# A first feed-forward with eight gated experts: bias products on four row groups, second projection behind the last expert bank

## The chip, the cores and the metric

The kernel runs on one core of a Trainium2 chip. The metric is the device time of one execution in microseconds (us), the median over several runs; lower is better. TensorE is the matmul engine, VectorE, ScalarE and GpSimd are the elementwise engines (DVE, ACT and POOL in the rows), SyncE (SP) issues most transfers.

## The reference

A two-layer transformer on 4 x 512 tokens of width 256, float32. The change touches the first layer's feed-forward, a dense mixture of experts:

```python
router_logits = x @ router_w + router_b          # 8 experts
top 2 of softmax(router_logits), renormalised -> gates (zero for the others)
expert_out = gelu(einsum('bsh,ehd->ebsd', x, expert_w) + expert_b)
combined   = einsum('bse,ebsd->bsd', gates, expert_out)
y          = combined @ out_w + out_b
x          = layernorm(x + y)
```

Before it stands an attention with 16 heads of width 16, behind it an attention with 16 heads of width 128 in 4 groups, and a second feed-forward with a capacity per expert. All 8 experts are computed for every token; the gates pick two.

## The kernel before

**Numbers.** Each float32 matrix is split into two bfloat16 parts, high and low, and a product is three matmuls (`mm3`, lines 350 to 355: high by high, high by low, low by high). The profile shows them as lines 353, 354 and 355.

**Tiles.** The 2048 tokens are 16 tiles (NT) of 128. The 8 experts of a tile are 8 x 256 = 2048 columns, four PSUM banks of 512: banks 4 to 7, two experts in each. `experts(t, p)` (line 502) computes bank p of tile t: it waits until the gelu of the same bank of tile t-1 has read it (`m["ge"]`), issues one bias product (line 506) with three rows of ones against three bfloat16 parts of the bias, and then six matmuls of 512 columns (two halves of the 256 inputs, three parts each). The bias is in `eb3`, rows 0 to 2 of a scratch region, 2048 columns wide.

**What follows a bank.** ScalarE applies the gelu (`gelu`, line 942) into `ge[p]`. VectorE (`mix`, lines 1284 and 1287) weighs experts 0 to 4 with their gates and adds them up; GpSimd does experts 5, 6 and 7 (`mix`, lines 1593 and 1598); VectorE joins both sums (`join_halves`, line 1293). TensorE transposes the combined tile ("cm", line 468), ScalarE and VectorE copy the transposed tile into high and low parts (lines 803 and 1092), and `second_project` (line 485) multiplies it with the output weights: six matmuls of 256 columns into bank 3. VectorE adds the result to the rows and takes their statistics (`joined(t, 2)`, lines 1197 to 1200), GpSimd forms the inverse deviation (`inverse_deviation`, lines 1577 and 1580), VectorE scales (`norm(t, 2)`, line 1206), and TensorE transposes the new rows ("x2") for the next layer.

**Three tiles at once.** A loop over steps n (line 593; its engines have the same loop at lines 958, 1336 and 1601) works on the experts of tile n, the second projection of tile n-1, the x2 transposes of tile n-2, and far ahead on the end of the attention: the first projection and norm of tile n+6 (`first_project`, `joined(n + 6, 1)`, `norm(n + 6, 1)`), its transposes "x1" of tile n+5, and the transposes "cc" of tile n+7. Tiles ahead end with step 9. At n = 3, 7, 11 (and before 0) a step also routes four tiles: logits on TensorE, softmax and top 2 on VectorE, with a table load of ScalarE before and after the exponential.

**Order.** All engines are programmed by hand in program order, with semaphores between them. Within a step it is:
- TensorE: x1 transposes; bank 0; logits (routing steps); x2 transposes; first projection; bank 1; cm transposes; cc transposes; bank 2; second projection; bank 3.
- ScalarE: x1 copy; gelu 0; x2 copy; gelu 1; cm copy; cc copy; gelu 2; gelu 3.
- VectorE: x1, x2 low parts; mix 0; joined(n+6, 1); cm, cc low parts; mix 1; norm(n+6, 1); joined(n-1, 2); mix 2; context; norm(n-1, 2); join_halves(n).
- GpSimd: inverse deviation for norm 1; mix 2; inverse deviation for norm(n-1, 2); mix 3; adding the output bias to rows (line 1618).

A turn waits until the low part of the turn before the last has been read (`hold(pe, m["tlo"], i - 1)`), so in a full step the cm transposes wait for join_halves and for the x1 low part behind it.

Step 16 has no experts: it starts the next layer's K, Q and V projections (`l1_project`), and the second projection of tile 15 stands before V. Step 17 holds the x2 transposes of tile 15. Then come the next layer's scores (line 646).

**The bias.** SyncE loads it as 16 rows of 128, GpSimd splits it into three parts (`eb_p`), and three copies by DMA (line 328) lay each part out as one row of 2048. TensorE waits for them at line 563, after the first attention.

Of the kernel before, what the change touches and what calls it, by code (L numbers as in the profile page):

```python
# [6 lines left out]
BF16 = mybir.dt.bfloat16  # L7
# [10 lines left out]
NT = NB * TT  # L18
# [105 lines left out]
def build(nc, x_tok_d, x_t_d, wqkv_d, wall_d, const_d, bp_d, outb_d, b2_d, rb_d, eb_d, rw0_d, rw1_d, b1_d, out_d):  # L124
    ctx = ExitStack()
    with ctx:
        def sb(name, shape, dt=F32):
            return ctx.enter_context(nc.sbuf_tensor(name, shape, dt))

        def sem(name):  # L130
            return ctx.enter_context(nc.semaphore(name))
# [12 lines left out]
        scr = sb("scr", [P, 16384])  # L144
# [5 lines left out]
        ones_b = sb("ones_b", [P, P], BF16)  # L150
# [52 lines left out]
        eb_f = scr[0:16, 6400:6528]  # L203
        eb_p = scr[0:16, 6528:6720].bitcast(BF16).rearrange("p (i d) -> p i d", i=3)
        eb_r = scr[0:16, 6720:6976].rearrange("p (i d) -> p i d", i=2)
        eb3 = scr[0:3, 15360:16384].bitcast(BF16)

        def tiles(base, n, width, dt=F32):
            return [scr[:, base + width * i:base + width * (i + 1)].bitcast(dt) if dt != F32
                    else scr[:, base + width * i:base + width * (i + 1)] for i in range(n)]  # L210
# [7 lines left out]
        ge = tiles(8192, 4, 512)  # L218
# [10 lines left out]
        bank = [ctx.enter_context(nc.psum_tensor(f"bank{i}", [P, 512], F32)) for i in range(8)]  # L229
# [12 lines left out]
        eb_moved = sem("eb_moved")  # L242
# [11 lines left out]
        def hold(eng, semaphore, value):  # L254

            if value > 0:
                eng.wait_ge(semaphore, value)

        def group_sems(p):
# [7 lines left out]
        m = {n: sem(f"mix_{n}") for n in (  # L267
            "rc", "cc", "tp", "thi", "tlo", "o1", "o2", "r1", "r2", "agg1", "agg2", "rstd1", "rstd2", "x1", "x2", "xb",
            "lg", "lgc", "lgd", "ex", "gates", "f", "ge", "mul", "pmul", "psum", "dve", "pool")}
# [21 lines left out]
        def _(sp):  # L291
# [32 lines left out]
            sp.wait_ge(ch_done, NCH)  # L324
            sp.dma_start(eb_f, eb_d).then_inc(ld_b, 16)
            sp.wait_ge(eb_ready, 1)
            for i in range(3):
                sp.dma_start(eb3[i:i + 1, :], eb_p[:, i, :]).then_inc(eb_moved, 16)

            def l1_turns(u):  # L330

# [18 lines left out]
        def _(pe):  # L350
# [134 lines left out]
            def second_project(t):  # L485
                pe.wait_ge(m["tlo"], TURNS.index(("cm", t)) + 1)
                hold(pe, m["r2"], t)
                project(bank[3][:, 0:E], tc_hi[t % 2], tc_lo[t % 2], OUTW).then_inc(m["o2"], 1)
# [12 lines left out]

            def experts(t, p):

                hold(pe, m["ge"], 4 * (t - 1) + p + 1)
                out = bank[4 + p][:, :]
                pe.matmul(out, ones_b[0:3, :], eb3[:, p * 512:(p + 1) * 512], start=True, stop=False)
                for k in range(KE):
                    cs = slice(EXPW + k * NX * E + p * 512, EXPW + k * NX * E + (p + 1) * 512)
                    last = mm3(out, tb_hi[t % TB][:, k * P:(k + 1) * P], tb_lo[t % TB][:, k * P:(k + 1) * P],
                               w_hi[:, cs], w_lo[:, cs], False, k == KE - 1)  # L510
                last.then_inc(m["f"], 1)
# [31 lines left out]
            for _ in range(WARM):  # L543
                pe.matmul(bank[7][:, :], ones_b[:, :], ones_b[:, :].unsqueeze(1).to_broadcast([P, TT, P]),
                          start=True, stop=True)
# [14 lines left out]


            pe.wait_ge(ch_done, NCH)
            pe.wait_ge(eb_moved, 48)
            pe.wait_ge(a["vc"], NH + 2)
            def l1_project(which, g, j=0):

# [26 lines left out]
            for n in STEPS[len(EARLY):]:  # L593
                here, ahead, behind = 0 <= n < NT, n + LEAD + 1, n - 1
                if 0 <= n + LEAD < NT:
                    turn_mix("x1", n + LEAD)
                if n == NT:

                    pe.wait_ge(m["ge"], 4 * NT)
                    l1_project("k", 0)  # L600
                if here:
                    experts(n, 0)
                if 0 <= n + 4 < NT and (n + 4) % TT == TT - 1:
                    logits((n + 4) // TT)
                if 0 <= n - 2:
                    turn_mix("x2", n - 2)

                routed = 0 <= n + 4 < NT and (n + 4) % TT == TT - 1
                if 0 <= ahead < NT and not routed:
                    first_project(ahead)  # L610
                if here:
                    experts(n, 1)
                if 0 <= ahead < NT and routed:
                    first_project(ahead)
                if 0 <= behind < NT:
                    turn_mix("cm", behind)
                if 0 <= n + LEAD + 2 < NT:
                    turn_mix("cc", n + LEAD + 2)
                if n == NT:
                    l1_project("q", 0, 0)  # L620
                if here:
                    experts(n, 2)
                if 0 <= behind < NT:
                    second_project(behind)
                if n == NT:
                    l1_project("v", 0)
                if here:
                    experts(n, 3)
            l1_project("q", 0, 1)


# [1067 lines left out]
```

## Time and profile before

| | |
|---|---|
| median of 3 runs | 1030.12 us (1030.11 to 1031.32) |
| the profiled execution | 1035.02 us, its span 1033.2 us |
| busy share of the span | TensorE 90%, VectorE 80%, ScalarE 61%, GpSimd 36% |
| mean granted TensorE clock | 0.973 |
| first attention | to 311.7 us |
| stage of the change, tile 0 to the next layer's scores | 324.4 to 497.3 us |
| starts of bank 0 of tiles 4, 5, 6, 7, 8 | 365.2, 378.0, 388.2, 398.6, 409.5 us |
| starts of bank 0 of tiles 12, 13, 14, 15 | 450.7, 461.2, 469.6, 477.9 us |

The starts of bank 0 are those of its bias products. A tile takes 10.4 us where a tile ahead is projected too, 12.8 with routing, and 8.4 at the end. In a row of the timeline the first number is the start in us from the span's start, the second the duration, then the engine, the line, the operation and what it writes and reads; a bracket tells how long the engine sat idle before it and who released it. The idle time of an engine that nobody waits for costs nothing.

### The profile page before, as it was taken

How to read it: one execution, taken by the hardware profiler on the slowest of the kernel's cores; microseconds unless marked ns; L12 is line 12 of the kernel's file. 1: busy time of each engine (PE TensorE's matmuls, PEld its weight loads, DVE VectorE, ACT ScalarE, POOL GpSimd, SP SyncE). 2: the span in 40 equal slices, each digit the busy share in tenths (PEclk: the TensorE clock that was granted, in tenths of full speed). 3: DMA queues.
4: the chain of work that ended last, by engine and by line, in shares of the span. 5: the costliest groups of instructions: out<-in, count | busy, mean ns of one | idle time of the engine just before them, and what ended most of it. 6: DMA issues, size and time to landing. Idle time of an engine off the chain costs nothing.

```text
span 1033.2 us, 23457 instructions
## 1 busy us (share of the span) xinstructions
PE 925.1 (90%) x8745; PEld 626.5 (61%) x8745; DVE 822.4 (80%) x2400; ACT 629.7 (61%) x1560; POOL 373.7 (36%) x605
## 2 busy tenths in 40 slices
PE   6888888887877988998899999999999999999996
PEld 4667676666663444433555566666666666667654
DVE  6999998989986687765799988888888888733566
ACT  6999998989862344343666655555555555432543
POOL 4333342530422545444233333333333333310085
PEclk8999999999986999999999999999999999999999
DMA  7202121100000000000266755555555655510001
GB/s 267 63 23 63 43 63 43 46 20 2 2 2 1 1 1 1 1 1 1 56 125 121 123 100 96 100 97 96 103 103 102 98 97 100 95 36 1 1 32 52
DMA packets 174626, 61.41 MB, mean 59 GB/s; under 512 B 169248, under 2 KB 170800, under 8 KB 174384
## 3 DMA queue, kind: packets, MB, share of 16 engines
q1 hardware_dynamic: 174512, 59.90, 28.7%
q8 instruction: 70, 1.15, 0.4%
q14 instruction: 44, 0.36, 0.1%
HBM read 15.83 MB, written 2.10 MB: 17 GB/s over the span
## 4 chain that ended last, share of the span: by engine, by line
PE 47%; DVE 31%; ACT 6%; POOL 5%; DMA 5%; issue 5%; SPq 0%; POOLq 0%; DVEq 0%; ACTq 0%
PE bank L353 11%; PE bank L355 11%; PE bank L354 11%; DVE s_sb L1135 7%; DMA pt_lo<-w_lo 5%; DVE pt_lo L1092 5%; DVE scr L1122 3%; DVE scr L1092 3%; PE bank L668 3%; PE bank L670 3%; PE bank L669 3%; DVE w_lo L1153 2%; ACT s_sb L850 2%; ACT scr L803 2%; POOL scr L1598 2%
## 5 line engine op out<-in xcount | busy, mean ns | idle before, releaser
L1135 DVE CUSTOM_DVE_ANT_0 s_sb<-bank,consts 128x512 f32<-128x512 f32 (+3 forms) x512 | 227.9, 481 | 23.3 <-PE bank L355 15.0
L852 ACT ACTIVATE s_sb<-s_sb,nm 128x512 f32<-128x512 f32 (+3 forms) x256 | 141.4, 553 | 103.8 <-DVE nm L1135 102.4
L353 PE MATMUL bank<-w_hi,scr 128*128 128x256 bf16 (+1 forms) x576 | 174.2, 302 | 5.1 <-DVE lg_sb L1299 2.6
L355 PE MATMUL bank<-w_hi,scr 128*128 128x256 bf16 (+1 forms) x576 | 173.6, 301 | 0.0
L354 PE MATMUL bank<-w_lo,scr 128*128 128x256 bf16 (+1 forms) x576 | 173.6, 301 | 0.0
L803 ACT ACTIVATE scr<-bank 128x256 bf16<-128x256 f32 (+4 forms) x256 | 120.2, 487 | 76.1 <-PE bank L670 44.5
L850 ACT ACTIVATE s_sb<-s_sb,nm 128x512 f32<-128x512 f32 (+3 forms) x256 | 141.2, 584 | 13.5 <-DVE nm L1135 13.4
L1628 POOL TENSOR_SCALAR wqkv_hi<-s_sb,rr 128x512 bf16<-128x512 f32 (+3 forms) x128 | 65.6, 532 | 141.7 <-DVE rr L1159 141.7
L1092 DVE TENSOR_TENSOR pt_lo<-bank,pt_hi 128x512 bf16<-128x512 f32 (+1 forms) x192 | 108.4, 592 | 7.6 <-ACT pt_hi L803 7.6
L1092 DVE TENSOR_TENSOR scr<-bank,scr 128x256 bf16<-128x256 f32 (+1 forms) x160 | 80.6, 525 | 40.8 <-ACT scr L803 40.4
L403 PE MATMUL bank<-scr 128*128 128x512 bf16 (+3 forms) x256 | 61.7, 306 | 50.9 <-DVE nm L1135 49.4
L1628 POOL TENSOR_SCALAR w_hi<-s_sb,rr 128x512 bf16<-128x512 f32 (+3 forms) x128 | 65.6, 532 | 105.2 <-DVE rr L1159 105.2
L803 ACT ACTIVATE pt_hi<-bank 128x512 bf16<-128x512 f32 (+1 forms) x192 | 96.4, 550 | 2.7 <-PE bank L449 2.7
L668 PE MATMUL bank<-pt_hi,w_hi 128*128 128x384 bf16 (+2 forms) x320 | 84.8, 275 | 10.6 <-DMA pt_lo<-w_lo 9.8
L942 ACT ACTIVATE scr<-bank 128x512 f32<-128x512 f32 x64 | 38.2, 597 | 86.0 <-PE bank L355 82.5
L669 PE MATMUL bank<-pt_lo,w_hi 128*128 128x384 bf16 (+2 forms) x320 | 87.9, 275 | 0.0
L353 PE MATMUL bank<-xt_hi,w_hi 128*128 128x512 bf16 x224 | 84.9, 379 | 1.7 <-ACT scr L1023 0.8
L355 PE MATMUL bank<-xt_hi,w_lo 128*128 128x512 bf16 x224 | 84.9, 379 | 0.0
L354 PE MATMUL bank<-xt_lo,w_hi 128*128 128x512 bf16 x224 | 84.9, 379 | 0.0
L670 PE MATMUL bank<-pt_hi,w_lo 128*128 128x384 bf16 (+2 forms) x320 | 84.6, 275 | 0.0
L353 PEld LDWEIGHTS bank<-w_hi,scr 128*128 128x128 bf16 x576 | 56.8, 99 | 43.3 <-issue 15.9
L449 PE MATMUL bank<-consts,s_sb 128*128 128x128 f32 x640 | 81.7, 275 | 0.0
(160 smaller groups left out, 2348.6 us busy)
## 6 DMA issues: line engine op xcount, KB each, us to landing
scr<-wall_in SPq DMA_DIRECT2D x19, 512.0 KB, 3.8
x_tok<-x_tok_in SPq DMA_DIRECT2D x1, 2048.0 KB, 9.8
scr<-x_t_in SPq DMA_DIRECT2D x3, 512.0 KB, 9.4
out<-x_tok SPq DMA_DIRECT2D x3, 512.0 KB, 2.6
scr<-wqkv_in SPq DMA_DIRECT2D x2, 384.0 KB, 4.0
pt_hi<-w_hi SPq DMA_TRANSPOSE x32, 3.3
pt_lo<-w_lo SPq DMA_TRANSPOSE x32, 3.4
pt_hi<-wqkv_hi SPq DMA_TRANSPOSE x32, 3.4
```

Of the source, the lines that this page charges most:

```text
L353: pe.matmul(out, l_hi, r_hi, start=start, stop=False, skip_group_check=check)
L354: pe.matmul(out, l_hi, r_lo, start=False, stop=False, skip_group_check=check)
L355: return pe.matmul(out, l_lo, r_hi, start=False, stop=stop, skip_group_check=check)
L668: pe.matmul(out, v1_hi[:, vs], hi, start=(kt, q0) == (0, 0), stop=False, skip_group_check=True)
L669: pe.matmul(out, v1_hi[:, vs], lo, start=False, stop=False, skip_group_check=True)
L670: last = pe.matmul(out, v1_lo[:, vs], hi, start=False, stop=(kt == TT - 1), skip_group_check=True)
L803: return act.activation(out, in_, ACT.Copy)
L850: last = act.activation(at, at, ACT.Exp, bias=nm[:, j % 2, qt:qt + 1], scale=-1.0)
L852: last = act.activation(at, at, ACT.Exp, bias=nm[:, j % 2, qt:qt + 1], scale=-1.0, accum_out=rs[:, j % 2, qt:qt + 1])
L1092: return dve.tensor_tensor(out, bank_cols, hi, ALU.subtract)
L1135: last = dve.tensor_tensor_reduce(s_sb[j % 2][:, S_OFF[qt]:S_OFF[qt] + w], bank[turn][:, col:col + w], mask[:, 512 - w:512], -scale, HUGE, ...
L1628: pool.tensor_scalar(ps_hi[j % 2][:, at], s_sb[j % 2][:, at], rr[:, j % 2, qt:qt + 1], 1.0, ALU.mult, ALU.mult).then_inc(c["row"], 1)
```

## The change

One bias product per bank becomes a group of four at the head of bank 0. The bias region is laid out anew: 12 row copies by DMA instead of three put the three parts of bank q's 512 columns into rows 32q to 32q+2, so that the four products read four different groups of 32 rows and are given the array's four row groups by `tile_position`. As all four banks are written at that point, bank 0 waits for all four gelus of the tile before (`4 * t`), and banks 1 to 3 for nothing. The second projection of the tile before is moved from between banks 2 and 3 to behind bank 3; in step 16 this puts it behind the V projection of the next layer.

```diff
-        eb3 = scr[0:3, 15360:16384].bitcast(BF16)
+        eb3 = scr[:, 15360:15616].bitcast(BF16)
...
-            for i in range(3):
-                sp.dma_start(eb3[i:i + 1, :], eb_p[:, i, :]).then_inc(eb_moved, 16)
+            for p in range(4):
+                for i in range(3):
+                    sp.dma_start(eb3[32 * p + i:32 * p + i + 1, :], eb_p[4 * p:4 * p + 4, i, :]).then_inc(eb_moved, 16)
...
             def experts(t, p):
 
-                hold(pe, m["ge"], 4 * (t - 1) + p + 1)
                 out = bank[4 + p][:, :]
-                pe.matmul(out, ones_b[0:3, :], eb3[:, p * 512:(p + 1) * 512], start=True, stop=False)
+                if p == 0:
+                    hold(pe, m["ge"], 4 * t)
+                    for q in range(4):
+                        rows = slice(32 * q, 32 * q + 3)
+                        pe.matmul(bank[4 + q][:, :], ones_b[rows, :], eb3[rows, :], start=True, stop=False,
+                                  tile_position=(32 * q, 0))
                 for k in range(KE):
...
-            pe.wait_ge(eb_moved, 48)
+            pe.wait_ge(eb_moved, 12 * 16)
...
                 if here:
                     experts(n, 2)
-                if 0 <= behind < NT:
-                    second_project(behind)
                 if n == NT:
                     l1_project("v", 0)
                 if here:
                     experts(n, 3)
+                if 0 <= behind < NT:
+                    second_project(behind)
```

## Rows read from the trace of the kernel before

**Rows 1.** The page, part 1: busy time, share of the span and instructions.
```profile
PE 925.1 (90%) x8745; PEld 626.5 (61%) x8745; DVE 822.4 (80%) x2400; ACT 629.7 (61%) x1560; POOL 373.7 (36%) x605
```
**Rows 2.** Waits, 324 to 486 us: who waited for whom, us, times, longest.
```profile
DVE scr L1293 <- POOL scr L1598: 29.9, 12, 3.5
```
**Rows 3.** Timeline of step 5, from one join_halves to the next.
```profile
381.77 0.93 DVE L1293 TENSOR_TENSOR scr<-scr 128x256 f32<-128x256 f32 x1 [2.37 <-POOL scr L1598]
...
383.18 0.74 PE L468 MATMUL bank<-consts,scr 128*128 128x128 f32 x4 [0.81 <-DVE scr L1092]
...
383.85 0.38 PE L506 MATMUL bank<-scr,ones_b 3*128 3x512 bf16 x1
...
384.17 0.39 PE L353 MATMUL bank<-w_hi,scr 128*128 128x512 bf16 x1
...
385.52 0.10 PEld L353 LDWEIGHTS bank<-w_hi,scr 128*128 128x128 bf16 x1 [0.38 <-DVE scr L1092]
...
386.08 0.27 PE L355 MATMUL bank<-w_hi,scr 128*128 128x256 bf16 x1
...
386.28 0.39 PE L506 MATMUL bank<-scr,ones_b 3*128 3x512 bf16 x1
...
387.12 0.40 DVE L1197 TENSOR_TENSOR x_tok<-bank,x_tok 128x256 f32<-128x256 f32 x1
...
389.42 0.61 POOL L1593 TENSOR_SCALAR scr<-scr,s_sb 128x256 f32<-128x256 f32 x1
...
392.14 0.93 DVE L1293 TENSOR_TENSOR scr<-scr 128x256 f32<-128x256 f32 x1 [2.37 <-POOL scr L1598]
```
**Rows 4.** Timeline of step 13, from one join_halves to the next.
```profile
464.61 0.42 DVE L1293 TENSOR_TENSOR scr<-scr 128x256 f32<-128x256 f32 x1 [2.45 <-POOL scr L1598]
...
465.46 0.38 PE L506 MATMUL bank<-scr,ones_b 3*128 3x512 bf16 x1
...
467.63 0.27 PE L355 MATMUL bank<-w_hi,scr 128*128 128x256 bf16 x1
...
467.94 0.42 DVE L1197 TENSOR_TENSOR x_tok<-bank,x_tok 128x256 f32<-128x256 f32 x1 [0.54 <-PE bank L355]
...
470.35 0.55 POOL L1593 TENSOR_SCALAR scr<-scr,s_sb 128x256 f32<-128x256 f32 x1 [0.24 <-ACT scr L942]
...
473.00 0.42 DVE L1293 TENSOR_TENSOR scr<-scr 128x256 f32<-128x256 f32 x1 [2.45 <-POOL scr L1598]
```
**Rows 5.** Timeline of step 0, ScalarE: the fourth gelu.
```profile
334.46 0.60 ACT L942 ACTIVATE scr<-bank 128x512 f32<-128x512 f32 x1 [1.12 <-PE bank L355]
```
**Rows 6.** Timeline of TensorE in step 8, behind a routing step.
```profile
413.20 0.44 PE L468 MATMUL bank<-consts,x_tok 128*128 128x128 f32 x2 [1.90 <-DVE x_tok L1206]
```
**Rows 7.** Timeline of steps 7 and 11 (routing): bank 2's bias product, and joined.
```profile
405.21 0.39 PE L506 MATMUL bank<-scr,ones_b 3*128 3x512 bf16 x1
...
408.25 0.42 DVE L1197 TENSOR_TENSOR x_tok<-bank,x_tok 128x256 f32<-128x256 f32 x1
...
446.56 0.38 PE L506 MATMUL bank<-scr,ones_b 3*128 3x512 bf16 x1
...
449.05 0.42 DVE L1197 TENSOR_TENSOR x_tok<-bank,x_tok 128x256 f32<-128x256 f32 x1
```
**Rows 8.** Timeline of step 16: second projection of tile 15, and joined.
```profile
491.82 0.27 PE L353 MATMUL bank<-w_hi,scr 128*128 128x256 bf16 x1
...
493.26 0.41 DVE L1197 TENSOR_TENSOR x_tok<-bank,x_tok 128x256 f32<-128x256 f32 x1
```
**Rows 9.** Timeline of SyncE's queue: the bias copies.
```profile
281.88 2.49 SPq L328 DMA_DIRECT2D scr<-scr  x3
```
**Rows 10.** Stretches: us, TensorE busy (x), granted clock, DMA share, GB/s.
```profile
414.00:418.00 4.00, 4.00 (x14) 0.57 0.00 0
...
491.00:496.00 5.00, 3.21 (x37) 1.00 0.00 0
```

## The prediction

> **What bounds the kernel now.** I read the page first: TensorE is busy for 90% of the span [rows 1]. That is no proof that it sets the pace, since overlapping matmuls are counted to their modelled ends, so I went to the only stage that the change touches, from the first expert bank at 324 us to the first scores of the next layer at 497 us. The waits there show VectorE waiting 29.9 us, at 12 of 16 tiles, for GpSimd's last addition of the gated experts [rows 2]. The timeline of one tile then shows the loop that repeats [rows 3]. Call J the start of join_halves(n), 381.77. VectorE runs on without a pause through the turned halves, the mix of banks 0 and 1, and norm(ahead), to joined(n, 2) at 387.12 = J + 5.35. Its statistics free GpSimd, whose rsqrt of the tile before stands in program order ahead of its mix of bank 3; that mix starts at 389.42, 2.30 after joined, and its four operations end in the next J, 392.14. The period is 10.37 us. TensorE enters this loop at one place only: joined(n, 2) needs the second projection of the tile. Its last matmul starts at 386.08 and takes 0.27, so it is there 0.77 us before VectorE wants it. TensorE itself waited 0.81 us before the cm transposes at 383.18: it has room.
>
> At the end of the stage it is different. From tile 10 on there is no tile ahead to project and normalise, VectorE is early, and joined starts 0.04 us after the projection's end (467.63 + 0.27, then 467.94) [rows 4]. GpSimd's mix starts at 470.35, released by the gelu of bank 3 after a wait of 0.24; with the 2.30 of the steady tiles the rsqrt would have allowed 470.24. Period 8.39 (464.61 to 473.00): here two paths, over the second projection and over bank 3, are 0.1 to 0.2 us apart, and both run over TensorE.
>
> **The change, part by part.**
>
> **Bias products.** Removed: a K=3 product at the head of each bank. Each stands 0.32 us ahead of its bank's first matmul (383.85, 384.17), where neighbours in a bank stand 0.217 apart; 64 of them. Added: four in a row per tile, in four row groups, ahead of bank 0. The trace has no such group. It costs at least one product, 0.32, and at most four of today's, 1.28; I take 0.6, near the low end: one product and three weight loads of 0.10 (385.52) behind it [rows 3]. TensorE thus does about 0.7 us less per tile. This takes nothing off the steady loop, as TensorE waits there anyway. Only its move out of banks 2 and 3 counts there: between the cm transposes and the second projection one bias product less is issued.
>
> The rows show that the product after a 256-wide one starts 0.20 later, not 0.11 (386.08, 386.28), and the next matmul again late. The Trainium skill (TensorEngine Tiling (Array Packing), Key Properties) says that a change of tiling mode drains TensorE, while different tiles run in parallel. No run here separates that drain from the rest. If both halves of the rule hold, the group pays for the switch once and is nearer to 0.4 than to 1.28; as this lies beside a wait, the sum would gain 0.2 us, at tile 0 alone.
>
> **The wait.** Bank 0 of tile t now waits for all four gelus of tile t-1, not for the first. Behind it in TensorE's order are bank 0, the x2 transposes, first_project and bank 1; VectorE and GpSimd wait for these only later. The cover is the second projection that now stands between bank 3 and this wait: bank 3 ends, the gelu takes 0.04 + 0.60 [rows 5], the projection 0.04 + 0.55 + 0.27 = 0.86 and (to tile 10) the x1 transposes 0.3. So it costs nothing. At tile 1 no projection stands there, and it costs about 0.45 us. If the cover were gone elsewhere, the 0.6 us would come out of idle time of TensorE, which I put at 1.8 us a tile afterwards (10.37 less the wait of 0.81 and the 0.7 saved is 8.86 of work in a tile of 10.62). In the routing tiles (3, 7, 11) ScalarE's table loads make the fourth gelu late; TensorE then waited 1.90 us for the x2 rows anyway [rows 6].
>
> **The second projection behind bank 3.** This is on the loop. With T for the start of today's bias product of bank 2 (383.85), the new order is: bank 2 and bank 3 without bias, 12 matmuls by 0.217 = 2.60; a step of 0.04 and five of 0.11 to the last matmul of the projection (385.52 to 386.08 now); 0.27 for it and 0.04 to VectorE, and 0.02 before the first. Joined can start at T + 3.52. It starts now at:
> - steady tiles 2, 5, 6: T + 3.27 (387.12 - 383.85 [rows 3]): 0.25 late each;
> - tiles 3, 7 (routing, 408.25 - 405.21 = 3.04 [rows 7]) 0.48; tiles 4 and 8 0.46 and tile 9 0.42 by the same difference in their rows, which repeat the pattern; tile 1 about 0.3;
> - tiles 10 and 12 to 15: T + 2.48 (467.94 - 465.46 [rows 4]): 1.04 late. GpSimd's mix then waits for the rsqrt, to 467.94 + 1.04 + 2.30 = 471.28 instead of 470.35: 0.9 each;
> - tile 11: 449.05 - 446.56 = 2.49 [rows 7], so 1.03, and VectorE is then busy without a wait up to join_halves: all of it.
>
> What is late moves the whole loop, J, the next cm transposes, the next tile, and is not won back, since nothing in the loop idles but TensorE.
>
> **Tile 0.** There TensorE is the bound: no projection lies in it, its fourth gelu at 334.46 waited for TensorE, and GpSimd and VectorE follow [rows 5]. Three products less at 0.32 (the one behind bank 0 runs before the clock has risen and is longer, some 0.45) against 0.3 more in the group: 0.8 earlier.
>
> **After the last tile** the projection also passes the V projection of the next layer: 24 matmuls of 128 columns, by half the 0.11 of those of 256: 1.32. The projection started from 491.82, and VectorE, busy with other work, took it up at 493.26 without a wait [rows 8]. Now it ends at 491.82 + 1.32 + 0.55 + 0.27, so VectorE starts at 494.0: 0.76 late, and the x2 transposes and last Q projection of the stage wait for it. The scores behind them start late by the same.
>
> **DMAs.** Twelve row copies instead of three on SP's queue, where three take 2.5 us from 281.9 on [rows 9]: they are out by 292 instead of 284.4. TensorE waits for them only behind the first attention, past 311 us, and SP's next copies belong to the next layer's attention: nothing. Without that gap it would be 7.5 us.
>
> **Sum.** Tiles 1 to 9: 0.3 + 3 x 0.25 + 2 x 0.48 + 2 x 0.46 + 0.42 = 3.4. Tiles 10, 12 to 15: 4.5; tile 11: 1.0; end: 0.8; tile 0: -0.8. In all +8.9 us, on the profiled execution 1035.02 to 1043.9, its span 1033.2 to 1042.1. That execution is 4.9 us above the median of 1030.12; I carry the difference over: **1039.0 us**. Bounds: T + 3.52 is good to 0.1 on 16 tiles, 1.6 each way; the group at 0.32 or 1.28 shifts tile 0 by -0.3 or +0.7.
>
> **Rivals.**
> 1. Not slower but faster: TensorE sets the pace and the time follows bank 3. Its place is tiles 10 and 12 to 15, which run almost without idle time of TensorE and where the gelu of bank 3 is today's last releaser. That bank now ends two bias products (0.36 each) and the projection (0.86) earlier, 1.5 us: five tiles give -7.6, tile 0 -0.8, the steady tiles 0: 1021.7. It decides if GpSimd's mix of bank 3 can start with that gelu, that is if the rsqrt of the tile before comes no later than 0.1 us after it does now. Against it: the code puts that rsqrt ahead of the mix, and it waits for the projection, which now has all of bank 3 before it. Chance 0.08.
> 2. The later projection is absorbed (the matmuls of banks 2 and 3 run closer, or the order of GpSimd's and VectorE's shared work shifts in its favour) in the steady tiles, but not in the last six: 4.5 + 1.0 + 0.8 - 0.8 = +5.5, 1035.6. Chance 0.2. With the last tiles at half of it too it would be no change; 0.05.
> 3. The clock. Within 1.5 us of the wait of 1.90 us TensorE fell from 2.4 to 1.2 GHz: a granted 0.57 over 414 to 418 us is 3.4 of 4 us at half clock [rows 6, 10], and it ended just as bank 2 began. Now TensorE idles more, some 0.6 to 0.9 before the x2 and 1.1 to 1.5 before the cm transposes in every tile. If a stretch of 3.4 us at 0.50 falls on banks 2, 3 and the projection, 1.7 us is lost. Three or four times is 5 to 7 us: 1044 to 1046. For it: the idle time. Against it: from 491 to 496 us matmuls fill only 3.21 of 5 us, and the clock stays whole [rows 10]. Chance 0.17.
> 4. The row groups don't overlap: the group costs 1.28. TensorE's idle time takes it, but for tile 0: 1039.5. It lies inside my range.
>
> **Numbers.** Forecast (with rival 4) 0.5, rival 1 0.08, rival 2 0.25, rival 3 0.17. A difference of 0.2%, 2 us, is about what can be told from none here. Slower: 0.5 + 0.17 + 0.2 = 0.87; same 0.05; faster 0.08. The range reaches from rival 2 less its bound, 1034, to rival 3, 1045; left out are rival 1, no change and more losses of clock.
>
> **What would show it.** The bias products start close together, once per tile; joined(n, 2) waits for TensorE in every tile and starts 3.5 us after bank 2; steady tiles take 10.6 us, the last ones 9.3 instead of 8.4; the fourth gelu comes early and GpSimd's mix of bank 3 waits for the rsqrt, not for it; the transposes of TensorE wait longer. Wrong if the last tiles take 8.4 us or less, if joined does not wait in the steady tiles, or if stretches at clock 0.50 lie in more tiles than three.

## The result, and the profile after

The changed kernel takes 1043.51 us in the median of four runs (1041.66 to 1052.69) against 1030.26 us of the kernel before on the same chip: ratio 1.0138 [1.0092, 1.0184], slower by 1.4%. The forecast was 1039.0 us with 1034 to 1045 around it. Run once more, on another chip, the same kernel gave 1047.96 us beside 1031.88, 1.0166 [1.0138, 1.0194]. The profiled execution took 1052.69 us with a span of 1050.9, which is 17.7 us longer than the span before. All line numbers of the new code are a few higher: the bias products are L510, the matmuls L354 to L356, the transposes L469, the gelu L947, join_halves L1298, joined L1202, norm L1211, the low parts L1097, the copy of the logits L1304, GpSimd's rsqrt L1585 and its mix L1598 and L1603.

The page, its busy times and the granted clock in 40 slices of some 26 us (the busy line answers to [rows 1]):

```profile
PE 922.9 (88%) x8745; PEld 632.8 (60%) x8745; DVE 823.3 (78%) x2400; ACT 632.3 (60%) x1560; POOL 372.0 (35%) x605
...
PEclk8999999999887989889899999999999999999999
```

The instructions are the same in number as before. TensorE's matmuls are busy for 2.2 us less, VectorE for 0.9 and ScalarE for 2.6 us more: most of the 17.7 us is waiting. The digits show the second thing to look at: of the six slices from 368 to 525 us four show 8, where all six of the kernel before show 9.

The timeline of step 5, from one join_halves to the next, answers to [rows 3] (start, us, engine, line, operation; in brackets the idle time before it and its releaser):

```profile
386.18 0.93 DVE L1298 TENSOR_TENSOR scr<-scr 128x256 f32<-128x256 f32 x1 [2.37 <-POOL scr L1603]
...
387.59 0.74 PE L469 MATMUL bank<-consts,scr 128*128 128x128 f32 x4 [1.33 <-DVE scr L1097]
...
388.17 0.38 PE L354 MATMUL bank<-w_hi,scr 128*128 128x512 bf16 x1
...
391.25 0.40 DVE L1211 TENSOR_SCALAR x_tok<-x_tok,mv,rstd 128x256 f32<-128x256 f32 x1
391.30 0.27 PE L356 MATMUL bank<-w_hi,scr 128*128 128x256 bf16 x1
391.61 0.42 DVE L1202 TENSOR_TENSOR x_tok<-bank,x_tok 128x256 f32<-128x256 f32 x1
...
392.08 0.40 PE L510 MATMUL bank<-scr,ones_b 3*128 3x512 bf16 x4
...
392.41 0.39 PE L354 MATMUL bank<-w_hi,scr 128*128 128x512 bf16 x1
...
396.65 0.93 DVE L1298 TENSOR_TENSOR scr<-scr 128x256 f32<-128x256 f32 x1 [2.36 <-POOL scr L1603]
```

The four bias products stand as one group, and bank 0's first matmul starts 0.33 us behind their start (392.08, 392.41); one product alone had taken 0.32. Joined starts at J + 5.43, 0.08 later than before. It has no wait of its own: VectorE's norm ends at 391.65 and the projection at 391.57. So VectorE and TensorE come to it together, and the period is 10.47 us where it was 10.37.

The timeline of step 13, one of the last tiles, answers to [rows 4]:

```profile
478.02 0.43 DVE L1298 TENSOR_TENSOR scr<-scr 128x256 f32<-128x256 f32 x1 [2.36 <-POOL scr L1603]
...
478.51 0.44 PE L469 MATMUL bank<-consts,scr 128*128 128x128 f32 x2 [1.05 <-DVE scr L1298]
...
481.92 0.27 PE L356 MATMUL bank<-w_hi,scr 128*128 128x256 bf16 x1
482.22 0.40 PE L510 MATMUL bank<-scr,ones_b 3*128 3x512 bf16 x4
482.23 0.42 DVE L1202 TENSOR_TENSOR x_tok<-bank,x_tok 128x256 f32<-128x256 f32 x1 [1.41 <-PE bank L356]
...
483.84 0.55 POOL L1585 TENSOR_TENSOR rstd<-var_e,neg_half 128x1 f32<-128x1 f32 x1
...
484.49 0.61 POOL L1598 TENSOR_SCALAR scr<-scr,s_sb 128x256 f32<-128x256 f32 x1
...
487.20 0.42 DVE L1298 TENSOR_TENSOR scr<-scr 128x256 f32<-128x256 f32 x1 [2.36 <-POOL scr L1603]
```

Joined waits 1.41 us for the projection, GpSimd's mix starts directly behind its rsqrt (483.84 + 0.55, then 484.49) and no longer behind a gelu, and the period is 9.18 us instead of 8.39.

What the forecast left out of its sum shows in the stretches of the same trace (window; length, TensorE busy and instructions; granted clock; DMA share, GB/s):

```profile
348.00:360.00 12.00, 8.51 (x67) 1.00 0.01 1
361.00:365.00 4.00, 4.00 (x14) 0.57 0.00 0
365.00:372.00 7.00, 3.18 (x21) 0.95 0.00 1
372.00:378.00 6.00, 5.92 (x20) 0.50 0.00 0
378.00:408.00 30.00, 24.33 (x157) 1.00 0.01 1
```

At a granted 0.50 TensorE runs at 1.2 GHz. The rows around it give the chain (timeline, steps 3 and 4):

```profile
360.05 0.27 PE L354 MATMUL bank<-w_hi,scr 128*128 128x256 bf16 x1 [2.08 <-DVE lg_sb L1304]
...
361.21 0.63 PE L354 MATMUL bank<-w_hi,scr 128*128 128x512 bf16 x1
...
366.27 0.43 DVE L1202 TENSOR_TENSOR x_tok<-bank,x_tok 128x256 f32<-128x256 f32 x1 [1.92 <-PE bank L356]
...
372.08 0.69 PE L469 MATMUL bank<-consts,x_tok 128*128 128x128 f32 x2 [3.90 <-DVE x_tok L1211]
```

In the routing tile TensorE waits 2.08 us. A microsecond later its clock falls, and the slow stretch lies on banks 2 and 3 (0.63 us a matmul instead of 0.38) ahead of the projection. Joined then waits 1.92 us. Everything behind it is late, the x2 rows too, for which TensorE waits 3.90 us. With the clock whole all along (e10_fill_end, below) bank 0 of tile 4 ends 9.03 us behind the start of join_halves of tile 2, and in the kernel before the x2 rows are there 10.69 us behind it: I estimate from these two that this wait would have been 1.7 us. A long wait can also come without a slow stretch ahead of it: in e2_move, below, TensorE waits 3.91 us at the same place. Behind the 3.90 us the clock is low again, over first_project, bank 1 and the start of bank 2 (to about 378), all ahead of the next joined. Tile 3 takes 15.70 us instead of 13.71 and tile 4 11.93 instead of 9.91. The same pair comes back in tiles 7 and 8; shorter stretches lie at tiles 10 and 12, and further ones on the next layer's projections in step 16 (506 to 511 us, at 0.50) and on the first work behind the stage.

Tile by tile, as sums of the time from one join_halves to the next, in us. "1 to 9" is from the one of tile 0 to the one of tile 9; "end" is from the one of tile 15 to its x2 transposes. The runs are told of below.

| | 1 to 9 | 10, 12 to 15 | 11 | end |
|---|---|---|---|---|
| before | 98.18 | 42.85 | 11.02 | 5.99 |
| after | 106.44 | 49.36 | 11.83 | 9.28 |
| e1_group | 98.34 | 40.31 | 11.01 | 6.00 |
| e2_move | 110.59 | 53.28 | 12.66 | 9.57 |
| e10_fill_end | 99.83 | 46.79 | 11.84 | 6.77 |

From before to after this is 8.26 + 6.51 + 0.81 + 3.29 = 18.9 us. Tile 0, from the first bias product to its join_halves, gives 1.4 back (13.37 to 11.95), but begins 1.6 later. That start moves between the profiles of kernels that are the same up to there (323.8 to 326.5), and 1.3 of the 1.6 us are there at the bias copies already (281.88 and 283.22), in the first attention, so I count it to nothing. With it the x2 transposes of tile 15 come 19.1 us later than before (495.77, 514.84). The span is only 17.7 us longer: 1.4 us are won back behind that point, and this was not followed up.

### The profile page after: what moved, and what is told of

Same layout as the page of the kernel before. It is cut to its first block, busy times and chain, and to the rows that moved or that the text cites. A ratio compares the mean times of both kernels' runs of the same rounds, so it can differ in the third digit from the quotient of the medians.

```text
span 1050.9 us, 23466 instructions
## 1 busy us (share of the span) xinstructions
PE 922.9 (88%) x8745; PEld 632.8 (60%) x8745; DVE 823.3 (78%) x2400; ACT 632.3 (60%) x1560; POOL 372.0 (35%) x605
## 4 chain that ended last, share of the span: by engine, by line
PE 54%; DVE 26%; ACT 6%; POOL 6%; issue 4%; DMA 3%; POOLq 0%; SPq 0%; DVEq 0%; ACTq 0%
PE bank L354 13%; PE bank L356 13%; PE bank L355 13%; DVE s_sb L1140 7%; DVE pt_lo L1097 4%; DVE scr L1127 3%; PE bank L673 3%; PE bank L675 3%; PE bank L674 3%; DVE scr L1097 3%; DMA pt_lo<-w_lo 2%; ACT s_sb L855 2%; POOL scr L1603 2%; ACT scr L808 2%; PE bank L404 2%
## 5 line engine op out<-in xcount | busy, mean ns | idle before, releaser
L354 PE MATMUL bank<-w_hi,scr 128*128 128x256 bf16 (+1 forms) x576 | 176.9, 307 | 6.9 <-DVE lg_sb L1304 4.7
L355 PE MATMUL bank<-w_lo,scr 128*128 128x256 bf16 (+1 forms) x576 | 176.5, 306 | 0.0
L356 PE MATMUL bank<-w_hi,scr 128*128 128x256 bf16 (+1 forms) x576 | 176.3, 306 | 0.0
L1097 DVE TENSOR_TENSOR pt_lo<-bank,pt_hi 128x512 bf16<-128x512 f32 (+1 forms) x192 | 108.4, 592 | 7.6 <-ACT pt_hi L808 7.6
L1097 DVE TENSOR_TENSOR scr<-bank,scr 128x256 bf16<-128x256 f32 (+1 forms) x160 | 80.7, 525 | 38.6 <-ACT scr L808 38.2
L354 PE MATMUL bank<-xt_hi,w_hi 128*128 128x512 bf16 x224 | 85.9, 384 | 1.0 <-ACT scr L1028 0.8
L356 PE MATMUL bank<-xt_hi,w_lo 128*128 128x512 bf16 x224 | 85.9, 384 | 0.0
L947 ACT ACTIVATE scr<-bank 128x512 f32<-128x512 f32 x64 | 38.0, 597 | 72.9 <-PE bank L356 72.8
L1582 POOL TENSOR_SCALAR var_e<-mv 128x1 f32<-128x1 f32 x64 | 16.8, 262 | 177.7 <-DVE mv L1205 104.1
```

The source lines that it names most:

```text
L354: pe.matmul(out, l_hi, r_hi, start=start, stop=False, skip_group_check=check)
L355: pe.matmul(out, l_hi, r_lo, start=False, stop=False, skip_group_check=check)
L356: return pe.matmul(out, l_lo, r_hi, start=False, stop=stop, skip_group_check=check)
L1097: return dve.tensor_tensor(out, bank_cols, hi, ALU.subtract)
```

## The experiments

**e1_group: the group alone.** The second projection is back between banks 2 and 3; the group and its wait stay.

```diff
                 if here:
                     experts(n, 2)
+                if 0 <= behind < NT:
+                    second_project(behind)
                 if n == NT:
                     l1_project("v", 0)
                 if here:
                     experts(n, 3)
-                if 0 <= behind < NT:
-                    second_project(behind)
```

> The changed kernel with the second projection back between banks 2 and 3 (in step 16 ahead of V): only the bias group and its wait for four gelus are left. My theory (the later projection on the loop and the clock cost the time, the group is cheap): joined(n, 2) starts about 0.4 us earlier after the cm transposes than in the kernel before, since the bias product of bank 2 is gone; the last tiles take about 8.1 us instead of 8.39, the steady ones about 10.37, the routing ones 13.7, and the whole is 1025 to 1029 us, faster than the kernel before. Rival (the wait for the fourth gelu, which now has only the x1 transposes or nothing as cover, is what costs): TensorE waits 0.3 to 0.65 us in each tile ahead of the group and the time stays at 1036 or more.

Measured: 1028.93 us in the median of 12 runs, 0.9976 [0.9966, 0.9986]: faster than both kernels. Its last tiles (timeline of step 13):

```profile
463.67 0.42 DVE L1298 TENSOR_TENSOR scr<-scr 128x256 f32<-128x256 f32 x1 [2.37 <-POOL scr L1603]
...
466.57 0.42 DVE L1202 TENSOR_TENSOR x_tok<-bank,x_tok 128x256 f32<-128x256 f32 x1
...
467.87 0.60 ACT L947 ACTIVATE scr<-bank 128x512 f32<-128x512 f32 x1 [1.35 <-PE bank L356]
...
468.52 0.39 PE L510 MATMUL bank<-scr,ones_b 3*128 3x512 bf16 x4 [0.69 <-ACT scr L947]
468.77 0.41 DVE L1211 TENSOR_SCALAR x_tok<-x_tok,mv,rstd 128x256 f32<-128x256 f32 x1 [0.72 <-POOL rstd L1585]
468.83 0.61 POOL L1598 TENSOR_SCALAR scr<-scr,s_sb 128x256 f32<-128x256 f32 x1
...
471.56 0.42 DVE L1298 TENSOR_TENSOR scr<-scr 128x256 f32<-128x256 f32 x1 [2.37 <-POOL scr L1603]
```

One bias product less, that of bank 2, lies between the cm transposes and the projection: joined comes at J + 2.90 instead of 3.33, and the period falls from 8.39 to 7.89, in five tiles 2.5 us. Tiles 1 to 9 stay (98.34, 98.18). Tile 0 is 2.1 us shorter in this profile (13.37, 11.23); five others with the same code in it gave 11.90 to 12.43, so how much of that an execution without a profile has is not known. Here nothing covers the new wait: TensorE idles 0.69 us ahead of the group for the fourth gelu (0.47 in the steady tiles), and a steady tile takes 10.42 instead of 10.37 us. So the wait costs TensorE idle time and at most 0.05 us of a steady tile.

**e2_move: the move alone**, in the kernel before, which keeps a bias product at the head of each bank.

```diff
                 if here:
                     experts(n, 2)
-                if 0 <= behind < NT:
-                    second_project(behind)
                 if n == NT:
                     l1_project("v", 0)
                 if here:
                     experts(n, 3)
+                if 0 <= behind < NT:
+                    second_project(behind)
```

> The kernel before with the second projection behind bank 3 and V, bias products as before, one at the head of each bank. My theory: joined(n, 2) then starts 4.2 us after the bias product of bank 2 instead of 2.5 (last tiles) or 3.3 (steady ones); last tiles 9.9 us, steady ones 11 us, in all about 8 us above the changed kernel without its stretches at half clock: 1045 to 1052 us. Rival (the wait for four gelus ahead of the group costs, the place of the projection is free): 1030 to 1033 us.

Measured: 1061.65 us, 1.0292 [1.0273, 1.0312]. That is 10 us beyond what I expected, and 14 to 18 us slower than the move together with the group (1047.96, 1043.51). A steady tile takes 11.32 us, 0.95 more than before, where with the group it takes 0.10 more: the bias products of banks 2 and 3, 0.32 and some 0.1 behind a 256-wide matmul each [rows 3], now stand ahead of the projection, and with them joined waits. One joined of a steady tile, and one of the longest waits of TensorE (timeline, steps 5 and 4):

```profile
373.61 0.44 PE L468 MATMUL bank<-consts,x_tok 128*128 128x128 f32 x2 [3.91 <-DVE x_tok L1206]
...
387.65 0.93 DVE L1293 TENSOR_TENSOR scr<-scr 128x256 f32<-128x256 f32 x1 [2.37 <-POOL scr L1598]
...
393.93 0.42 DVE L1197 TENSOR_TENSOR x_tok<-bank,x_tok 128x256 f32<-128x256 f32 x1 [0.85 <-PE bank L355]
```

Joined comes at J + 6.28 and waits 0.85 us. And the clock is lost, behind the wait of 3.91 us among others (stretches, columns as above):

```profile
368.00:373.00 5.00, 1.70 (x7) 1.00 0.00 0
374.00:377.00 3.00, 2.67 (x12) 0.61 0.00 0
```

The two parts of the change are not a sum: e1_group is 2.8 us below the kernel before and e2_move 29.9 above, and both together are 13 to 16 above.

**e3_vorder: the projection of tile 15 ahead of the V projection**, all else as after.

```diff
                 if n == NT:
+                    second_project(behind)
                     l1_project("v", 0)
                 if here:
                     experts(n, 3)
-                if 0 <= behind < NT:
+                if 0 <= behind < NT - 1:
                     second_project(behind)
```

> The changed kernel, but in step 16 the second projection of tile 15 stands ahead of the V projection again. My theory: joined(15, 2) starts about 0.8 us earlier after the cm transposes of tile 15 and so do the next layer's scores; nothing ahead of it changes. Rival (VectorE is busy there anyway): the stretch from the last join_halves to the first scores is the same as in the changed kernel.

One execution: span 1046.3 at a clock of 0.961. The tiles are as after to 0.02 us; from the last join_halves to the last x2 transposes it takes 8.44 us instead of 9.28, 0.84 less, where 0.76 had been predicted. The last joined starts at J + 5.04 instead of 6.76. TensorE then waits 1.74 us for the x2 rows instead of 2.56, and behind them its clock stays whole, where in the changed kernel it was 0.83 over 516 to 522 us: the next matmul that TensorE waits for comes 12.06 us after these transposes (513.62, 525.68) instead of 13.57 (514.84, 528.41). So some 1.5 of the other 3.8 us of the span's difference lie there. The rest is not placed.

**e4_fill: is it the clock?** As after, with products of no use into columns that nothing reads, in TensorE's idle places of tiles 2 to 15: 3 or 30 of 256 columns ahead of the x2 transposes, 8 or 16 ahead of the cm transposes. They write columns that the work around them doesn't use, and wait for nothing that it doesn't wait for.

```diff
+            def filler(n, count):
+
+                if n < 2:
+                    return
+                hold(pe, m["r2"], n - 1)
+                for _ in range(count):
+                    pe.matmul(bank[3][:, 256:512], ones_b[:, :], ones_b[:, :].unsqueeze(1).to_broadcast([P, 2, P]),
+                              start=True, stop=True)
...
+                if here:
+                    filler(n, 30 if n in (4, 8, 12) else 3)
...
+                if here:
+                    filler(n, 16 if routed else 8)
```

> The changed kernel with added matmuls whose result nobody reads, where TensorE waits: 3 of 256 columns ahead of the x2 transposes (30 in tiles 4, 8 and 12) and 8 behind bank 1 (16 in routing tiles), from tile 2 on. They add nothing to the work and keep TensorE busy. My theory (half-clock stretches behind long waits fall on banks 2, 3 and the projection and cost some 6 us in the profiled execution, 4 in the median): granted clock 1.00 through tiles 2 to 15, routing tiles 14.2 us instead of 15.7, the whole 1038 to 1040 us, and the spread between executions (1041.7 to 1052.7) shrinks. Rival (the clock is only a by-product of waiting): the stretches go and the time stays at 1042 to 1044, or rises by what the added matmuls take.

Measured: 1040.26 us, 1.0087 [1.0072, 1.0102], which is 8.5 us above the kernel before on the same chip; the unfilled kernel was 13.3 and 16.1 us above it, so 5 and 8 us are won, and its span is 12.5 less. More work on TensorE made the kernel faster. Over tiles 2 to 15 the granted clock is 1.00 (345 to 494 us); only step 16 still has a low stretch (0.66 over 496 to 500 us). Tiles 3 and 4 fall from 15.70 and 11.93 us to 13.68 and 10.42.

**e5_serial: the same four products on one row group**, in e1_group, with the bias in three rows by three copies as in the kernel before.

```diff
-                        rows = slice(32 * q, 32 * q + 3)
-                        pe.matmul(bank[4 + q][:, :], ones_b[rows, :], eb3[rows, :], start=True, stop=False,
-                                  tile_position=(32 * q, 0))
+                        pe.matmul(bank[4 + q][:, :], ones_b[0:3, :], eb3[:, q * 512:(q + 1) * 512], start=True, stop=False)
```

> The kernel of e1_group (group of four at the head of bank 0, projection between banks 2 and 3), but all four products read rows 0 to 2 and so use one row group, with the bias laid out as in the kernel before. My theory (the four overlap only because of their row groups): from the first product of the group to the first matmul of bank 0 it takes about 0.97 us instead of 0.33. In tiles with idle time of TensorE that costs nothing; in the last ones, where TensorE waits 0.21 us before the cm transposes, 0.4 to 0.5 us each, so that they take 8.3 instead of 7.88: about 2 to 3 us above e1_group in all. Rival (the row groups do nothing, one product costs 0.1 to 0.3 in either form): the group takes the same as in e1_group and so does the kernel.

Measured: 1031.01 us, 0.9994 [0.9982, 1.0007]: no gain over the kernel before is left. Timeline, head of step 13:

```profile
463.60 1.03 PE L508 MATMUL bank<-scr,ones_b 3*128 3x512 bf16 x4 [0.69 <-ACT scr L944]
464.56 0.39 PE L353 MATMUL bank<-w_hi,scr 128*128 128x512 bf16 x1
```

One behind the other the four take 0.96 us, on four row groups 0.33: a factor of 2.9. The Trainium skill (TensorE: Matmul & The Clock Gate, Part 3) gives 3.07 for four products of 32 rows and 512 columns on four row groups; this case agrees with it, for three rows each. Tiles 13 to 15 take 8.18 us here and 7.89 in e1_group, so 0.3 of the 0.63 us come through, 0.9 us in these three. Tile 0 is 3.0 us longer (14.27, 11.23), but a low clock lies on it (0.50 over 328 to 334 us), and the two are not separated. So the overlap of the row groups is shown by the rows; what it is worth in the time of the kernel is not.

**e6_move_fill: e2_move with the same filler.**

> The kernel of e2_move with added matmuls that nobody reads, from tile 2 on: 3 of 256 columns ahead of the x2 transposes (30 in tiles 4, 8, 12), 5 behind bank 1 (12 in routing tiles). My theory: most of e2_move's 30 us is the later projection (steady tiles 11.3, last tiles 10.0 us), and 5 to 6 us is half-clock stretches behind the waits of 3.9 us: tile 4 falls from 11.87 to about 11, tile 8 from 13.11 to 11, tile 12 from 12.29 to 10.5, the whole to 1055 to 1057 us. Rival (the clock is all of what exceeded my sum): 1048 us.

Measured: 1054.14 us, 1.0231 [1.0211, 1.0251]. A steady tile still takes 11.32 us and tiles 3 and 7 14.9, as in e2_move; tiles 4 and 8 fall from 11.87 and 13.11 us to 10.80 and 10.75. So without the bias group the move costs 18.8 us in the tiles (170.88 against 152.05) at a whole clock. The median fell by 7.5 us, a little more than expected.

**e7_warm0: five and six products ahead of the x1 transposes of steps -1 and 0**, in e1_group, to raise the clock before tile 0.

```diff
+                for _ in range({-1: 5, 0: 6}.get(n, 0)):
+                    pe.matmul(bank[7][:, :], ones_b[:, :], ones_b[:, :].unsqueeze(1).to_broadcast([P, TT, P]),
+                              start=True, stop=True)
```

> The kernel of e1_group with 5 and 6 matmuls of 512 columns that nobody reads, ahead of the x1 transposes of steps -1 and 0, where TensorE waits 3.8 and 2.5 us and runs at half clock up to about 329 us, into tile 0. My theory: the clock has risen before bank 0 of tile 0, tile 0 is bound by TensorE, and join_halves of tile 0 comes about 2 us earlier: 1026 to 1027.5 us. Rival (tile 0 is bound by ScalarE's table load and VectorE's routing, or the clock does not rise in time): the time of e1_group, or up to 0.5 us more.

Measured: 1028.76 us, 0.9976 [0.9964, 0.9988], the same as e1_group and above the 1026 to 1027.5 that I had expected. The clock is whole from 325 us on, but tile 0 takes 10.92 us instead of 11.23, no more: with TensorE early, its x1 transposes of step 1 wait 1.18 us for VectorE.

**e8_after: the changed kernel once more**, to see whether its spread is chance.

> The changed kernel once more, unaltered. My theory: most executions at 1041 to 1048 us, and those above 1045 have a mean granted clock of 0.96 or less; in the profile the excess lies in tiles 3, 4, 7, 8, 10 and 12 as in the first one. Rival (something outside this stage, the twelve copies or the first attention, makes the spread): the tiles' lengths repeat those of the first profile and the difference lies elsewhere.

Measured: 1047.96 us in the median; its four executions took 1052.98, 1043.95, 1048.8 and 1047.12 us at clocks of 0.961, 0.972, 0.96 and 0.965. In the second profile every tile from 1 on has its length of the first to 0.02 us, and the stretches at half clock stand in the same places. Both profiled executions are the longest of their kernel. The others are 4 to 11 us shorter, and all but one have a higher mean clock (0.965 to 0.975 against 0.958 and 0.961), so they seem to have fewer stretches. But the one of 1048.8 us has 0.96 and the one of 1047.12 has 0.965, above the 0.96 that I had expected for it: the mean clock alone doesn't tell. Which stretches they lack is not known.

**e9_before_fill: the control**, filler in tiles 3, 4, 7 and 8 of the kernel before.

> The kernel before with added matmuls that nobody reads where its own half-clock stretches arise: 14 of 256 columns ahead of the x2 transposes in tiles 4 and 8, 8 behind bank 1 in tiles 3 and 7. My theory: the stretches at 370 and 414 us vanish, and as they ended where bank 2 began, nothing is gained: tiles 3, 4, 7 and 8 keep 13.7 and 9.9 us and the ratio to the kernel before is 0.999 to 1.001. The added matmuls are then free by themselves, and what they gained in e4_fill was clock that the later projection had lost. Rival (the added matmuls help in themselves, or the kernel before loses to its stretches too): 2 to 4 us faster.

Measured: 1031.97 us beside 1031.84, 1.0006 [0.9995, 1.0017]. Its stretches at a low clock [rows 10] are gone (1.00 over 331 to 496 us) and no tile is shorter by more than 0.05 us: 98.11 us for tiles 1 to 9 against 98.18. So this filler, 14 products in tiles 4 and 8 and 8 in tiles 3 and 7, is free, and the kernel before lost next to nothing to those stretches: they end where bank 2 begins. The 30 and 8 of e4_fill in tiles 4 and 8 are more than this control has, and they are not free (next experiment).

**e10_fill_end: e4_fill, with 18 instead of 30 products in tile 12 and 18 and 20 more in steps 16 and 17.** The change without loss of clock, as near as the runs come to it.

> The kernel of e4_fill, with 18 added matmuls instead of 30 in tile 12 (where 30 took longer than the wait) and 18 and 20 more in steps 16 and 17, ahead of the transposes of tile 15. My theory: tile 12 takes 9.2 us instead of 9.93, and joined(15, 2) comes at most 4.3 us after the last join_halves instead of 5.9 (3.5 in the kernel before), since banks and projections of step 16 no longer run at half clock: 1037.5 to 1039 us, some 2 us below e4_fill and 6 to 8 us above the kernel before, which is then the price of the later projection alone. Rival (the end of the stage is bound by VectorE and ScalarE): the time of e4_fill, 1040.

Measured: 1037.68 us, 1.007 [1.0047, 1.0092]; span 1037.7 us. The clock is whole over the stage (stretches; columns as above):

```profile
348.00:360.00 12.00, 11.29 (x95) 1.00 0.01 1
360.00:378.00 18.00, 17.07 (x120) 1.00 0.01 1
378.00:408.00 30.00, 28.06 (x195) 1.00 0.01 1
408.00:454.00 46.00, 41.59 (x291) 1.00 0.00 1
454.00:504.00 50.00, 45.58 (x298) 1.00 0.01 1
```

Its last tiles (timeline of step 13; line numbers again higher):

```profile
468.10 0.42 DVE L1321 TENSOR_TENSOR scr<-scr 128x256 f32<-128x256 f32 x1 [2.37 <-POOL scr L1626]
...
472.30 0.42 DVE L1225 TENSOR_TENSOR x_tok<-bank,x_tok 128x256 f32<-128x256 f32 x1 [1.41 <-PE bank L356]
...
474.56 0.61 POOL L1621 TENSOR_SCALAR scr<-scr,s_sb 128x256 f32<-128x256 f32 x1
...
477.28 0.42 DVE L1321 TENSOR_TENSOR scr<-scr 128x256 f32<-128x256 f32 x1 [2.37 <-POOL scr L1626]
```

Period 9.18, and the wait of 1.41 us of joined is there as after: in these tiles what is left is the later projection alone. In tiles 4 and 8 it is not. There the 30 products ahead of the x2 transposes took longer than the wait that they fill, and with the 8 behind bank 1 they push the cm transposes (timeline of step 4):

```profile
371.51 0.42 DVE L1321 TENSOR_TENSOR scr<-scr 128x256 f32<-128x256 f32 x1
...
372.12 1.04 PE L530 MATMUL bank<-ones_b 128*128 128x256 bf16 x8
...
373.00 0.60 PE L469 MATMUL bank<-consts,scr 128*128 128x128 f32 x4
```

The same place in e1_group:

```profile
371.87 0.42 DVE L1298 TENSOR_TENSOR scr<-scr 128x256 f32<-128x256 f32 x1
...
372.77 0.74 PE L469 MATMUL bank<-consts,scr 128*128 128x128 f32 x4 [1.52 <-DVE scr L1097]
```

They start at J + 1.49 behind filler instead of J + 0.90 (so in the kernel before too), 0.59 later, and joined of tile 4 waits 0.45 us. So up to 0.5 us each of tiles 4 and 8 are the filler's own, and the later projection costs up to 1.0 us less than e4_fill and e10_fill_end show.

## Why the prediction was right or wrong

The sign, the place and the mechanism held: the projection behind bank 3 makes joined late, GpSimd's rsqrt and mix follow it, and the loop follows them. The 1039.0 us came out 4.5 us too low, 9 by the second measurement. That the time lies no farther off is in part luck: the sum for the projection was 3 us too high, and the loss of clock, which the sum did not hold, was 7 to 10 us. By its own steps, with e10_fill_end as the change at a whole clock:

- **Tiles 10, 12 to 15**, predicted 4.5: 3.94 (46.79 less 42.85), 0.79 a tile. Joined came at J + 4.21 against 3.33, 0.88 late instead of 1.04, and the mix follows 2.26 behind it, not 2.30. **Tile 11**, predicted 1.03: 0.82.
- **Tiles 1 to 9**, predicted 3.4: 1.65. The mis-sized term is T + 3.52. Without its bias product bank 2 starts 0.58 behind the cm transposes (387.59, 388.17) instead of 0.67 to the old bias product [rows 3], and joined 3.44 behind that (391.61). That is 0.17 of the 0.25 in a steady tile, and then VectorE is busy until joined anyway: "joined(n, 2) waits for TensorE in every tile" is wrong there. Of the 0.10 that is left, 0.05 is there with the group alone (10.42 in e1_group). In tiles 3 and 7 joined is 0.30 late, and the interval with it no longer: 13.70 against 13.71. That "what is late is not won back" is wrong for the routing tiles. Tiles 4 and 8 have 0.50 each, predicted as 0.46, but up to all of it is the filler's, as shown above: with the cm transposes at J + 0.90 and joined 3.88 behind them, as in e10_fill_end, TensorE would be there at J + 4.78, and VectorE comes at J + 4.89 in any case. By this estimate tiles 1 to 9 cost 0.65 us and not 1.65. Tile 9 has 0.25 instead of 0.42.
- **The end**, predicted 0.76: 0.78 (6.77 less 5.99), and 0.84 by e3_vorder.
- **Tile 0**, predicted -0.8: -0.9 in e10_fill_end (13.37, 12.43) and -1.3 to -2.1 in the other profiles with the group on four row groups and this tile's code unchanged; the clock rises within this tile. The group at 0.6 us was mis-sized: it costs 0.33, the lower bound.
- **The new wait**, predicted at nothing from tile 2 on and 0.45 at tile 1: the group waits 0.40 there (timeline, head of step 1), and in the changed kernel for 1.17 us at tile 12, behind ScalarE's table load, which comes out of idle time. Even where the cover is gone, in e1_group, 0.47 us of waiting cost at most 0.05 us of a steady tile.

```profile
335.30 0.39 PE L510 MATMUL bank<-scr,ones_b 3*128 3x512 bf16 x4 [0.40 <-ACT scr L947]
```

- **The DMAs**, predicted at nothing: 7.55 us on SP's queue (next fence), out by 290.8, and no instruction waits for their end.

```profile
283.22 7.55 SPq L329 DMA_DIRECT2D scr<-scr  x12
```

These terms sum to 1.65 + 3.94 + 0.82 + 0.78 - 0.94 = 6.2 us, and the median of e10_fill_end is 5.8 above the kernel before (1037.68, 1031.84). The forecast had 8.9 for the same: some 3 too much, and up to 4 if the filler's own 1.0 is taken off.

**The clock**, carried beside the forecast as rival 3 at 0.17, is the rest, and it happened on top of the later projection, as that rival had it. In the profiled execution it cost 167.63 - 158.46 = 9.2 us in the tiles and 9.28 - 6.77 = 2.5 at the end. In the medians it cost 7 and 10 us, each taken against the kernel before on its chip (13.3 and 16.1 us above it, less the 5.8 of e10_fill_end), and up to 1.0 more by the filler's own price. The rival had 5 to 7, as three or four times 1.7; there were stretches in six tiles and in step 16. That is more than the three tiles which the prediction gave as a sign that it is wrong, and joined that does not wait in the steady tiles was another of its signs. What rival 3 got wrong is the cause. It looked to the small waits of every tile; those of a steady tile (0.47 and 1.33 us) left the clock whole. The falls follow waits of 1.99 to 3.90 us in the routing tiles and around them, and a fall makes the next wait longer: 2.08, then 3.90 where I estimate 1.7 at a whole clock. That a slow stretch makes the wait that brings the next one was nowhere in my sum.

That the parts are not a sum has little to do with the clock. At a whole clock the move costs 18.8 us in the tiles with a bias product at each bank (e6_move_fill) and 6.4 with the group (158.46 less 152.05), since two bias products, 0.84 us a steady tile, leave the path to the projection. The slow stretches come on top: 5.7 us in e2_move (176.53 less 170.88), 9.2 in the changed kernel. In e1_group they cost nothing. The cover of the gelu is gone and TensorE idles in a steady tile as much as after (0.47, 1.30 and 0.31 before its groups), but the projection comes early, so its longest waits in and behind the routing tiles are 1.42 to 1.88 us, and the clock is whole over all of tiles 2 to 15.

Rival 1, faster by way of bank 3's gelu, did not hold with the projection behind bank 3: GpSimd's mix went on waiting for the rsqrt, as argued against it. The group alone shows that the other path was worth something: with joined 0.43 us earlier, a last tile is 0.5 us shorter. Rival 2, absorbed in the steady tiles only, at 5.5 us, was nearer to the structure than my forecast: at a whole clock its 5.5 us would have been the best number. Rival 4 was wrong by e5_serial: the row groups overlap.

What stays open: how much clock an execution without a profile loses and at which tiles; what the later projection costs in tiles 4 and 8 with neither slow stretches nor filler; and what in the first attention moves the start of the stage from profile to profile.

## What to carry to other kernels

Where a change makes an engine wait longer, look at TensorE's clock in the stretches behind its longest waits, and ask what work would lie on a slow stretch: here the stretches on slack work cost nothing, and those on the producer of the critical row cost 12 us in the profiled execution. Filling such waits with products that nobody reads is a cheap test of it, if the filler is shorter than the wait: some idle time left in front of the next instruction that counts shows that it is. And measure the parts of a change by themselves: the half that paid 2.8 us was hidden under one that cost more than its whole gain.

## What the runs showed that I had not expected

Adding 259 matmuls in idle places (e4_fill, 3% of the 8745) made the changed kernel 5 to 8 us faster. A microsecond behind a wait of 2.08 us TensorE's clock was at 1.2 GHz for some 3.4 us; after waits of 1.66 and 1.52 us in e1_group it stayed at 2.4 GHz. The length of one wait does not settle it: 1.90 us in the kernel before was followed by 1.2 GHz [rows 6, 10], 1.88 us in e1_group (456.26) was not, and neither was 2.56 us in e4_fill (503.26; clock 1.00 over 503 to 514 us). And the places of the slow stretches were the same in both profiles of the changed kernel, to 0.02 us of tile length, while its executions differ by 9 us.
